# Edge messages built as per-group outer products in a four-layer graph network, with a reordered edge list and smaller edits

## The reference

```python
# layer 0: weighted neighbour sum        z = segment_sum(x[src] * w, row) @ W
# layer 1: per edge, two batch norms     h = relu(bn(concat(x[row], x[col]) @ W1 + b1)); h = relu(bn(h @ W2 + b2)); segment_sum(h, row)
# layer 2: two graph convolutions        agg = segment_sum(h[src] * norm, dst)
# layer 3: message passing with a weight matrix per edge
out = h = relu(n_feat @ lin0_w.T + lin0_b)
eh  = relu(e_feat @ en1_w.T + en1_b)                    # [edges, 128]
w_e = (eh @ en2_w.T + en2_b).reshape(-1, 32, 32)        # a 32x32 matrix for each edge
for _ in range(6):
    msg = einsum('ei,eio->eo', out[src], w_e)
    agg = segment_sum(msg, dst, 12500) + conv_bias
    out = h = gru_cell(relu(agg), h, wih, whh, bih, bhh)
```

## Time and profile before

| | us |
|---|---|
| median of three runs | 42725.9 |
| the profiled execution | 42514.04 |
| its span | 42512.1 |
| keys (120 to 786) | 666 |
| order_src, order_dst | 2474, 2540 |
| l0, l1a | 3100, 2960 |
| l1b, l1c | 450, 930 |
| l2a, l2b | 2740, 2730 |
| first l3m, first l3g | 3810, 120 |

### The profile page before, as it was taken

The page is one execution under the profiler, slowest core; times in us unless marked ns, Lnnn a source line. Parts: engine busy times, 40 slices in busy tenths (PEclk is TensorE's granted clock), DMA queues, the critical chain, the costliest instruction groups (busy, mean ns, idle before and its releaser), DMA issues. The chain is left out here.

```text
span 42512.1 us, 515826 instructions
## 1 busy us (share of the span) xinstructions
PE 30160.5 (71%) x99425; PEld 18121.0 (43%) x99426; DVE 29047.4 (68%) x63440; ACT 11318.4 (27%) x26426; POOL 30972.7 (73%) x31499
## 2 busy tenths in 40 slices
PE   5222234444465222249999999999999999999999
PEld 5332323333365222234444444444444444444444
DVE  7333322221155222249999999999999999999999
ACT  0000001111110000014444444444444444444444
POOL 1666655555503665669998999899899989998997
PEclk8555556655555555569999999999999999999999
DMA  1110012210031010011111111111111111111111
GB/s 45 41 41 24 20 35 62 62 34 21 21 76 23 12 12 12 12 25 46 46 45 44 46 45 45 45 46 45 44 46 45 46 44 46 45 46 44 45 46 42
DMA packets 1365766, 1669.90 MB, mean 39 GB/s; under 512 B 847196, under 2 KB 1012047, under 8 KB 1252303
## 3 DMA queue, kind: packets, MB, share of 16 engines
q1 hardware_dynamic: 664232, 1115.69, 8.2%
q0 software_dynamic: 669696, 495.09, 7.3%
q10 hardware_dynamic: 31680, 57.69, 0.4%
HBM read 1393.98 MB, written 274.47 MB: 39 GB/s over the span
## 5 line engine op out<-in xcount | busy, mean ns | idle before, releaser
L1706 PE MATMUL l3m_p_w<-en,l3m_hid 128*128 128x512 f32 x42240 | 20965.3, 619 | 656.8 <-DVE l3m_prod L1772 398.8
L1756 DVE TENSOR_REDUCE l3m_xg<-l3m_prod 128x32 f32<-128x1024 f32 x10560 | 12858.1, 1218 | 168.6 <-POOL l3m_prod L1637 0.8
L1628 POOL DMA_INDIRECT l3m_xg<-wide_table,l3m_mt x10560 | 10341.0, 979 | 2395.8 <-issue 2033.1
L1637 POOL TENSOR_TENSOR l3m_prod<-l3m_rest,l3m_xg 128x384 f32<-128x384 f32 x10560 | 10673.0, 1011 | 281.9 <-ACT l3m_rest L1683 93.7
L1706 PEld LDWEIGHTS l3m_p_w<-en,l3m_hid 128*128 128x128 f32 x42240 | 7164.5, 189 | 6865.7 <-issue 5224.6
L1683 ACT COPY l3m_rest<-l3m_p_w 128x384 f32<-128x384 f32 x10560 | 5050.6, 478 | 12815.6 <-PE l3m_p_w L1706 12187.2
L1768 DVE TENSOR_TENSOR l3m_prod<-l3m_p_w,l3m_xg 128x512 f32<-128x512 f32 x10560 | 7196.1, 681 | 429.2 <-PE l3m_p_w L1706 257.4
L1718 PEld LDWEIGHTS l3m_p_sum<-l3m_xg,l3m_apart 128*125 128x125 f32 x21120 | 3965.2, 188 | 5090.7 <-issue 2742.2
L1671 ACT ACTIVATE l3m_apart<-iota_lo,l3m_mt 128x125 f32<-128x125 f32 x10560 | 4238.6, 402 | 0.5 <-DMA l3m_mt<-dst_meta 0.5
L1718 PE MATMUL l3m_p_sum<-l3m_xg,l3m_apart 128*125 128x64 f32 x21120 | 3473.9, 246 | 23.0 <-DVE l3m_xg L1756 23.0
L858 POOL DMA_INDIRECT l2a_xg<-table,l2a_mt x1760 | 1676.7, 953 | 2443.5 <-DMA l2a_mt<-dst_meta 1896.8
(11 more groups left out here) (328 smaller groups left out, 22546.9 us busy)
## 6 DMA issues: line engine op xcount, KB each, us to landing
l3m_hid<-hid_t SPq DMA_DIRECT2D x660, 1024.0 KB
l3m_xg<-wide_table,l3m_mt POOLq DMA_INDIRECT x10560
hid_t<-l_hid SPq DMA_DIRECT2D x110, 1024.0 KB, 4.1
order_src_bk<-dst_bucket SPq DMA_DIRECT2D x52, 808.0 KB
order_dst_bk<-src_bucket SPq DMA_DIRECT2D x52, 808.0 KB
by_dst<-order_src_empty SPq DMA_DIRECT2D x28, 1071.0 KB, 24.4
l_rec<-by_dst SPq DMA_DIRECT2D x110, 272.0 KB
l_xg<-table,l_mt POOLq DMA_INDIRECT x1760
```

The source lines that it names most:

```text
L1628: pool.indirect_dma_start(xg[s][:, j, 0:2 * D], None, wide_table[:, :], bass.IndirectOffsetOnAxis(ap=mt[s][:, j, 0:1].bitcast(I32), axis=0 ...
L1637: pool.tensor_tensor(o_i(prod[j % RING][:, OWN:HD]), o_i(rest[j % RING][:, :]), state_of(s, j, REST), ALU.mult).then_inc(pooled, 1)
L1706: ins = pe.matmul(p_w[j % 2][:, c * 512:(c + 1) * 512], hid[s][:, j * P:(j + 1) * P], en2[:, c * 512:(c + 1) * 512], start=True, stop=True)
L1756: dve.tensor_reduce(xg[s][:, j, 2 * D:3 * D], o_i(prod[j % RING][:, :]), AX, ALU.add).then_inc(msgs, 1)
```

## The change

**The edge list for dst.** Nodes are now grouped by eight: group (l, d) with d = bucket // 8 holds up to 8 slots; 125 x 13 groups. Each group is padded to subtiles of 32 edges. Four subtiles make a quad of 128 edges: NBLK = 86 blocks of 24 quads, 2064 quads. `order("src", ...)` is replaced by `order_groups` (a rank by group, with a pairwise mask on DVE and 16 dependent steps a chunk between PE and ACT). In-degrees are now counted in `order("dst", ...)` instead of in `keys`.

**The message sum.** For a group of edges the sum over edges of msg is rearranged: first an outer product over the 32 edges of a subtile, outer[k, (i, slot)] = sum_e eh[e, k] * state[e, i] * hit[e, slot], then one product with en2 over k and i. So the edge's matrix never exists. The new l3m, cut to its core:

```diff
-                            for c in range(2):
-                                ins = pe.matmul(p_w[j % 2][:, c * 512:(c + 1) * 512], hid[s][:, j * P:(j + 1) * P],
-                                                en2[:, c * 512:(c + 1) * 512], start=True, stop=True)
+                        def times(b, k, j):
+                            for q in range(2):
+                                for x in range(2):
...
+                                    for c in range(2):
+                                        rows = slice((2 * x + c) * SUB, (2 * x + c + 1) * SUB)
+                                        ins = pe.matmul(half(t, x)[:, c, :, q * SLOTS:(q + 1) * SLOTS],
+                                                        eh[k][rows, 2 * j + q, :], spread[(2 * t + q) % RING][rows, :, :],
+                                                        start=True, stop=True)
+                        def mix(k, n):
+                            for c in range(4):
+                                ins = pe.matmul(p_pair[c * D:(c + 1) * D, 0:PAIRS], en2_i[:, 4 * n + c, :],
+                                                outer[k % 2][:, 4 * n + c, :], start=n == 0, stop=n == D // 4 - 1,
+                                                skip_group_check=True)
-                                dve.tensor_tensor(o_i(prod[j % RING][:, 0:512]), o_i(p_w[j % 2][:, 0:512]),
-                                                  state_of(s, j, 512), ALU.mult)
...
-                            dve.tensor_reduce(xg[s][:, j, 2 * D:3 * D], o_i(prod[j % RING][:, :]), AX,
-                                              ALU.add).then_inc(msgs, 1)
+                                dve.tensor_tensor(spread[(2 * t + q) % RING][:, :, :],
+                                                  xg[k][:, 2 * j + q, 0:D][:, :, None].broadcast_to([P, D, SLOTS]),
+                                                  p_hit[:, at:at + SLOTS][:, None, :].broadcast_to([P, D, SLOTS]),
+                                                  ALU.mult).then_inc(spreads, 1)
+                            dve.tensor_copy(outer_of(k, j)[:, 1], half(t, 0)[:, 1]).then_inc(dve_moved, 1)
+                            act.copy(outer_of(k, j)[:, 0], half(t, 0)[:, 0]).then_inc(act_moved, 1)
...
+                            act.copy(outer_of(k, j)[:, 2:4], half(t, 1)).then_inc(act_moved, 1)
-                            pool.tensor_tensor(o_i(prod[j % RING][:, OWN:HD]), o_i(rest[j % RING][:, :]),
-                                               state_of(s, j, REST), ALU.mult).then_inc(pooled, 1)
+                                    pool.wait_ge(spreads, b * QB + (k * SET + j + 1))
+                                    pool.sem_inc(begun, 1)
+                                    pool.indirect_dma_start(
+                                        xg[k][:, j, :], None, wide_table[:, :],
                                        bass.IndirectOffsetOnAxis(ap=mt[k][:, j, 0:1].bitcast(I32), axis=0)).then_inc(rows_in[k], 16)
```

**Other edits.** The convolution sums, `keys` and the degrees in `order_dst`:

```diff
-        gather_sum("l2a", dst_meta, 2, table, False, off_d, ACC)
+        dst_sum("l2a", table)
...
-                        dve.tensor_tensor(hit_lo[s][:, :, :], iota_b16[:, None, 0:LO].broadcast_to(wide),
-                                          lo16[1][:, cols][:, :, None].broadcast_to(wide), ALU.is_equal)
...
+                                for to, of, n in ((one_lo, d_lo, LO), (one_b, d_b, NB)):
+                                    ins = dve.tensor_tensor(to[:, :, :], p_iota[:, None, 0:n].broadcast_to([P, CC, n]),
+                                                            of[s][:, :, None].broadcast_to([P, CC, n]), ALU.is_equal)
...
+                            for t in range(CC):
+                                ins = pe.matmul(p_deg[0:LO, 0:NB], one_lo[:, t, :], one_b[:, t, :],
+                                                start=False, stop=True, skip_group_check=True)
```

`keys` keeps one of its three masks a group of 16 columns (the bucket of src). In `dst_sum` POOL gathers 2064 quads with four sets of six buffers. The loads of `l1b` get four buffers, and those of `l1c` wait for less:

```diff
-            mt = [ph.sb(f"mt{s}", [P, G, SR]) for s in range(2)]
-            h = [ph.sb(f"h{s}", [P, GD]) for s in range(2)]
+            mt = [ph.sb(f"mt{r}", [P, G, SR]) for r in range(RING)]
+            h = [ph.sb(f"h{r}", [P, GD]) for r in range(RING)]
...
-                            sp.wait_ge(summed, g + 1)
+                            sp.wait_ge(hits, g + 1)
```

More of the change, by code:

```diff
@@ L513, in build @@
+        order_groups()
         TMP = sb("TMP", [LO, W])
@@ L829, in _ @@
[L829 to L847 removed]
+                        net.start_sp(sp)
@@ new lines, in _ @@
+                        fetch(0, 0, True)
+                        fetch(0, 1, True)
+                        with nc.allow_non_contiguous_dma(reason="one word of each subtile's first record"):
+                            for c in range(4):
+                                sp.dma_start(sub_key.rearrange("(q c) -> c q", c=4)[c:c + 1, :],
+                                             by_dst[c * SUB:c * SUB + 1, 0:NQ, 1]).then_inc(keys_kept, 16)
+                        with sp.Fori(0, NI - 1) as i:
+                            for s in range(2):
+                                fetch(i + 1, s, True)
+                                net.store(sp, i, s)
@@ L968, in _ @@
                             fetch(i * 2 + s, s)
+                    with nc.allow_non_contiguous_dma(reason="keys by subtile"):
+                        sp.dma_start(own[:, :], sub_key.rearrange("(b n) -> n b", n=SB)).then_inc(own_in, 16)
                 @block.gpsimd
@@ new lines, in _ @@
+                        block_of(0, first=True)
+                        with sp.Fori(1, NBLK) as b:
+                            block_of(b)
+                        sums.fetch(sp, NBLK - 1)
+                        rows = wide_table[0:N, :].rearrange("(l b) f -> l b f", b=NB)
+                        for q in range(Q):
+                            sp.wait_ge(kept, q + 1)
+                            sp.wait_ge(b_kept, q + 1)
+                            sp.dma_start(rows[:, 4 * q:4 * q + 4, :], state[:, 4 * q:4 * q + 4, :]).then_inc(state_out, 16)
@@ new lines, in _ @@
+                        sums.start_pe(pe)
+                        pe.sem_inc(hits, 1)
+                        pe.sem_inc(outers, OUTERS)
+                        pe.sem_inc(mixed, MIXED)
+                        pe.sem_inc(biased, BIASED)
+                        block_of(0, first=True)
+                        with pe.Fori(1, NBLK) as b:
+                            block_of(b)
+                        mix_begin(NBLK, 0)
+                        for j in range(TWOS):
+                            mixes(SETS - 1, j)
```

1541 lines of the change are left out of this document (1067 added, 474 removed).

## The result

The changed kernel took 51235.2 us (median of 4 runs, 51211 to 51250), the kernel before 42725.4 us beside it: ratio 1.199, 95% interval 1.197 to 1.201. Forecast were 38400 us. The experiments then met six chips, each once. On four of them (numbers 1, 4, 5, 6) the kernel before takes 42508 to 42712 us and the changed one, run on chip 1, 50322 us (ratio 1.184, 1.182 to 1.186). On two (8, 15) the kernel before takes 39854 and 39895 us and the changed one, run on chip 8, 33276 us (ratio 0.835, 0.8325 to 0.8374). I call them the slow and the fast kind; the comparison above was made on one that behaves like the slow kind. Since no chip was met twice, I cannot say whether the kind belongs to the chip or to the hour.

What follows compares the result with a forecast made beforehand. PE and DVE filled l3m, POOL's gathers and scatters paced most else; PE would set l3m's new pace. From 42514 us, -4100 (l3m) and -250 (other stages) give 38164, plus 212 for run median: 38400 us; eight-in-ten range 34800 to 43900.

Steps and rivals of the forecast that it cites:

- the floor that I gave POOL: l3m, POOL: with its product gone, one gather a quad remains, 2064 x 1.25 = 2580 us a step at least.
- The array: l3m, PE: a quad costs 0.86 us outer products, 0.43 mixing, 0.13 bias and join, 0.09 shape changes: 1.51 us.
- POOL is the bound, and PE's loads run side by side too: Rival, l3m: step 2580 + 130 us, total 35200 us; 36400 at 1.35 us a quad; chance 0.34, nearly POOL-bound included.
- Passes block each other: Rival, l3m, PE: only two of four strips side by side, 1.94 to 1.98 us a quad, total 44200 us; chance 0.15.
- The change does something else in l3m, a wait of its own above 1.9 us: Rival, l3m: an unspecified wait above 1.9 us, no total given; chance 0.02.
- keys: Stage keys: three masks per 16 columns become one and DVE's adds go, -470 us of 666.
- Both orders: order_dst +300 us for added masks and products, order_groups +500 us for masks, pairs and PE's 16 steps a chunk.
- l0: Stage l0: same gathers, the network's products regrouped, between -300 and +200 us, taken as -100 us.
- l2a and l2b: Stages l2a, l2b: 2064 gathers at 1.25 us plus some 30 us, against 2740 and 2730 us: -130 us each.
- l1b: Stage l1b: four load buffers take away waits for loads, -120 us of 450.
- l1c: Stage l1c: DVE is busy 705 of 930 us, so -100 us.
- the six steps: l3m with its updates: six times 3117 + 130 us, 19480 us against 23580 us, -4100 us.

## Why the prediction was wrong

**The step that failed** is the floor that I gave POOL: "one gather a quad: 2064 x 1.25 = 2580 us, a floor", beside which PE was to work at its own pace. Gathers cost 1.25 us each as predicted (1946 us busy in every loop). But I took a gather to cost its own engine alone. On the slow kind, a burst longer than about 3 us takes nearly everything from the others: counted over the 338 full bursts of the first loop, 28.8 records of PE pass per us in the first 3 us and 5.2 in the 5.5 us after that, against 2 x 43336/2494 = 34.8 in the loop without gathers. The change does two things at once there. It takes away POOL's product, which stood between two gathers, and it triples PE's records, from 12 a tile in 2.165 us to 42 a quad. A set of six quads needs 252 records: some 87 pass in the first 3 us, 29 in the next 5.5 us, and the remaining 136 need 6.3 us, since PE then runs at 21.8 records per us. That is 0.63 of 34.8, and the granted clock of these stretches is 0.62 on average. Together 14.8 us, 2.46 us a quad. So of the 1.25 us a quad above the loop without gathers, the starved 5.5 us a set give 0.78 us (at the full rate 191 records would have passed in them, and the 162 that are lacking are 4.7 us), and the lower clock afterwards another 0.4 us (136 records in 6.3 instead of 3.9 us). That split is worked out from the trace and not tested by a run of its own; nor did any run put work back on POOL between two gathers.

The evidence lay in the rows that I had. The earlier trace rows show PE with one pass each 2 us and the reason "issue" while POOL scatters. I carried that rhythm into the two orders, where it is, and called it a matter of those stages. I never asked what l3m would look like once its gathers too came without a pause. On the fast kind the forecast fails as well: 33276 us lie below its 34800 us, because PE does a quad in less than I gave it, and the stages before l3m are shorter.

**The array.** The forecast's parts are seen on the fast kind, where two quads take this:

```profile
17800.52 1.15 PE L2389 MATMUL l3m_p_outer<-l3m_spread,l3m_eh 32*128 32x256 f32 x16
...
17801.60 1.18 PE L2404 MATMUL l3m_p_pair<-l3m_outer,en_i 128*32 128x192 f32 x24
...
17802.71 1.15 PE L2389 MATMUL l3m_p_outer<-l3m_spread,l3m_eh 32*128 32x256 f32 x16
```

Sixteen passes of 256 columns, 0.41 us each by their group, are through in 1.08 us with the change of shape: four side by side, and their four loads too. That is 0.54 us a quad, where I had 0.86 + 0.045, because I let the loads go one by one at 0.11 us. The mixing takes 24 passes in 1.11 us, so 64/24 x 1.11/6 = 0.49 us a quad (forecast 0.43 + 0.045). Without gathers a quad is 2494/2064 = 1.21 us in all, for my 1.51.

**The rivals.** "POOL is the bound, and PE's loads run side by side too" is what happens on the fast kind: 2690/2064 = 1.30 us a quad, between its 1.25 and 1.35 us. Its total of 35200 us was still 1900 us too high, because there the stages before l3m are shorter as well. "Passes block each other" is wrong on both kinds: the three rows above could not be if a pass waited for the one before, and on the slow kind the sixteen passes of 22120.33 take the same 1.15 us at the full clock. The Trainium skill states that matmuls start and end in program order (TensorE: Matmul & The Clock Gate, Part 3, "What overlaps and what doesn't"); that is a rule of order, and the wait of one strip for another I read into it. By the rows the order costs nothing of what I gave it. My rival for the other side thus had the right sign and a wrong mechanism; its limit is 1.86 us a quad by its own sum, not 1.87. "The change does something else in l3m, a wait of its own above 1.9 us" had a chance of 0.02, and is what came.

**The other terms**, forecast and measured in the two profiled executions of the first comparison: keys -470, -446 us. Both orders +800, +409 us; on the fast kind they take 4564 us in all, less than the 5117 us of before on the slow kind, so the rhythm of the earlier trace rows is of this kind of chip too. l0 -100, +304 us, and 2276 us on the fast kind, near the 2200 us of its gathers. l2a and l2b -130 each, +495 and +578 us: 2664 and 2651 us became 3159 and 3229 us, and on the fast kind they take 2672 us each, where I had forecast 2610. l1b -120, -129 us, l1c -100, -47 us. From the last mixing product of one loop to the first of the next pass 131 us, for my 130. l1a, to which I gave no change, +73 us. The sum of the terms that I forecast, +1160 us, is 1410 us off my -250 us; the six steps, 31160 us for 19480, are 11700 us off. These terms move between chips of the slow kind too: on chip 1, where both kernels were traced, the orders are +304, l0 +80, l2a +504 and l2b +536 us.

**What stays open.** The trace shows two things while gathers run. PE and SP stand still at instructions that wait for no semaphore (PE inside one row of products, SP at register moves of 697 ns); and a step of PE's semaphore arrives late, 22.9 us after the product in l2a, where ACT has hardly an instruction to execute. Whether these are one effect or two is open, and so is how much of l3m's loss belongs to each. By the trace it is not the loading of program code. The Trainium skill has it that a sequencer streams its instructions by itself and that crossing from one block of them to the next is mostly hidden (Runtime: NRT & Kernel Launch, Instruction fetch mechanics); the slow kind does not disagree, since the two instruction queues in its trace carry no packet between 20203 and 25164 us, that is in all but the first 0.1 ms of the first loop. And what makes a chip of one kind or the other no run here tells.

## What to carry to other kernels

An engine that is "off the path" by its own time can still hold up the others: before taking away work that stands between gathers, look in the trace for stages where gathers already come in a row, and see what the other engines' short instructions do there. A change that multiplies small instructions should be timed on more than one chip, because here one pair of kernels gave 1.199 and 0.835. Where gathers must run beside much other work, keep their bursts short.

## What the runs showed of the hardware

- Two kinds of chip, or of times: the kernel before takes 42508 to 42725 us or 39854 to 39895 us, with nothing between, and runs of one kernel on one chip agree within 0.3%.
- Four products on separate strips of 32 rows, or into separate strips of 32 columns, run side by side with their loads: 16 passes of 256 columns in 1.08 us, 24 of 192 columns in 1.11 us.
- On the slow kind POOL's indirect gathers starve the other engines (5080 us a loop); 128 rows of 256 bytes, loaded by SP at the same points, do nothing to PE (2513 us). PE's records come back 1.2 to 1.4 us after POOL's last gather instruction has ended, when the last rows have landed.
- While gathers run there, a register move of SP takes 697 ns in the median for 29 ns on the fast kind, and in one case a step of PE's semaphore arrives 22.9 us late.
- After 5.4 us in which PE did 29 records, it ran 6.4 us at 0.58 of the clock (between its levels of 1.2 and 2.4 GHz), though it was busy 6.2 of them.
